# One wait per transpose, one signal per normalisation, and a mask tile moved by 64 bytes

## The reference, cut to what matters

```python
h = jnp.maximum(_layernorm(x, axis=-1), 0.0)
# _direction, for each relation r of a direction:
#   sum_r (adj == r) @ ((h W.T + b_r) * sigmoid(h W.T Wg.T + bg_r))
out = _direction(h, W_fwd, Wg_fwd, ..., adj, rels)             # relations 2 to 40
out = out + _direction(h, W_bwd, Wg_bwd, ..., adj_t, rels)
out = out + _direction(h, W_loop, Wg_loop, ..., adj_t, rel1)   # relation 1
return x + jax.nn.relu(out)
```

## Time and profile before

| | |
|---|---|
| median of three runs | 104.29 us (104.07 to 104.54) |
| the profiled execution's own time | 104.14 us |
| its span | 102.4 us |
| TensorE clock | full speed, 0.999 of it |
| PE busy | 96.5 us, 94% |
| DVE busy | 90.3 us, 88% |
| ACT busy | 90.3 us, 88% |
| POOL busy | 83.8 us, 82% |

### The profile page before, as it was taken

One profiled execution on the slowest core, in us unless ns is written; L12 is line 12 of the kernel. 1 busy time (PEld: TensorE's weight loads), 2 busy tenths in 40 slices (PEclk: granted clock), 3 DMA queues, 4 the chain that ended last, 5 costly groups with the idle time before them and its releaser, 6 DMA issues.

```text
span 102.4 us, 2495 instructions
## 1 busy us (share of the span) xinstructions
PE 96.5 (94%) x802; PEld 92.5 (90%) x802; DVE 90.3 (88%) x197; ACT 90.3 (88%) x148; POOL 83.8 (82%) x158
## 2 busy tenths in 40 slices
PE   5988899999999999999999999999999999999960
PEld 2657798999999999999999999999999999999950
DVE  2289899999999999999999999999998588877661
ACT  5068889989999999999999989998999989898890
POOL 2275999999999999999999999999999999960000
PEclk9999999999999999999999999999999999999999
DMA  2899999999999999999999999999933341506345
GB/s 63 249 313 292 293 290 290 293 294 288 274 313 304 321 321 324 301 324 333 335 328 333 317 339 322 304 312 312 315 100 109 92 113 55 156 15 197 102 137 170
DMA packets 50288, 25.45 MB, mean 249 GB/s; under 512 B 866, under 2 KB 50276, under 8 KB 50276
## 3 DMA queue, kind: packets, MB, share of 16 engines
q1 hardware_dynamic: 50000, 25.17, 88.0%
q10 hardware_dynamic: 276, 0.13, 0.4%
HBM read 16.91 MB, written 8.39 MB: 247 GB/s over the span
## 4 chain that ended last, share of the span: by engine, by line
PE 80%; DMA 7%; DVE 4%; SPq 3%; ACT 3%; issue 1%
PE psum L827 25%; PE psum L805 14%; PE psum L806 14%; PE psum L810 14%; PE psum L792 13%; DMA x_all<-in_x 7%; ACT junk L467 2%; SPq L253 2%; DVE stats L554 1%; DVE xn L571 1%; DVE vals L587 1%; DVE hT_lo L597 1%; SPq L269 0%; SPq L270 0%; ACT gate L461 0%
## 5 line engine op out<-in xcount | busy, mean ns | idle before, releaser
L366 POOL TENSOR_SCALAR xn<-x_all,mean_neg,rstd 128x128 f32<-128x128 f32 x96 | 42.4, 456 | 0.5 <-issue 0.3
L805 PE MATMUL psum<-w_hi,hT_hi 128*128 128x256 f32 x128 | 34.3, 301 | 0.7 <-ACT hT_hi L427 0.3
L434 ACT ACTIVATE psum<-bias_all 128x1024 f32<-128x1024 f32 x32 | 33.0, 1032 | 0.7 <-DVE vals L587 0.6
L827 PE MATMUL psum<-vals,mask 128*128 128x128 f32 x256 | 33.6, 275 | 0.0
L806 PE MATMUL psum<-w_lo,hT_hi 128*128 128x256 f32 x128 | 31.6, 280 | 0.0
L827 PEld LDWEIGHTS psum<-vals,mask 128*128 128x128 f32 x256 | 31.1, 191 | 0.0
L554 DVE BATCH_NORM_STATS2 stats<-x_all 128x6 f32<-128x256 f32 x64 | 24.0, 420 | 3.5 <-DMA x_all<-in_x 3.5
L587 DVE TENSOR_TENSOR vals<-psum,gate 128x512 f32<-128x512 f32 (+1 forms) x33 | 21.9, 665 | 4.0 <-ACT gate L461 3.8
L805 PEld LDWEIGHTS psum<-w_hi,hT_hi 128*128 128x128 f32 x128 | 24.1, 188 | 1.5 <-issue 0.9
L348 POOL TENSOR_TENSOR rstd<-var_eps,minus_half 128x16 f32<-128x16 f32 (+2 forms) x11 | 24.5, 2224 | 0.1
L806 PEld LDWEIGHTS psum<-w_lo,hT_hi 128*128 128x128 f32 x128 | 24.2, 189 | 0.0
(11 more groups left out here) (38 smaller groups left out, 34.5 us busy)
## 6 DMA issues: line engine op xcount, KB each, us to landing
adj_all<-in_adj SPq DMA_DIRECT2D x16, 512.0 KB, 6.5
x_all<-in_x SPq DMA_DIRECT2D x15, 512.0 KB, 6.7
out<-x_all SPq DMA_DIRECT2D x14, 512.0 KB, 6.3
out<-x_all SPq DMA_DIRECT2D x3, 256.0 KB, 2.3
x_all<-in_x SPq DMA_DIRECT2D x2, 256.0 KB, 3.0
out<-x_all ACTq DMA_DIRECT2D x1, 128.0 KB, 2.5
out<-x_all SPq DMA_DIRECT2D x1, 128.0 KB, 2.6
w_raw<-in_L_gnn_W_loop SPq DMA_DIRECT2D x1, 64.0 KB, 2.4
```

The source lines that it names most:

```text
L366: last = pool.tensor_scalar(xn[:, g % XN, j * D:j * D + D], x_all[:, g * GC + j * D:g * GC + j * D + D], mean_neg[:, b % BATCH_SLOTS, k:k ...
L434: nc.scalar.activation(prod_ps[s].rearrange("p g a d -> p g (a d)"), bias_all[:, :, :].rearrange("p a d -> p (a d)").unsqueeze(1) .to_broa ...
L805: nc.tensor.matmul(to, hi, w_hi[:, :], start=False, stop=False, skip_group_check=True)
L827: last = nc.tensor.matmul(to[:, j * D:j * D + D], mask[:, g % MASKS, j * N:j * N + N], vals[:, s, j * D:j * D + D], start=True, stop=True)
```

## The change

Three things change.

1. Every normalisation instruction signals, on all three engines, and the counters count graphs: `pool_groups` and `dve_groups` become `pool_graphs` and `dve_graphs`, sums of the shares.
2. In `turn_rows` each transpose waits for its own graph's normalisation. The wait for the PSUM slot now comes first. The graphs of VectorE (or ScalarE) are transposed first, those of GpSimd last.
3. `minus_half` is allocated behind `mean_neg`. So `mask`, `stats`, `var_eps`, `rstd` and `mean_neg` move down by 64 bytes and begin at multiples of 128; what lies behind stays where it was.

```diff
-        minus_half = sb("minus_half", [128, BATCH])
         mask = sb("mask", [128, MASKS, GROUP * N])
...
         mean_neg = sb("mean_neg", [128, BATCH_SLOTS, BATCH])
+        minus_half = sb("minus_half", [128, BATCH])
...
-        def pool_groups(g):
-            return sum(pool_share(k) > 0 for k in range(g))
+        def pool_graphs(g):
+            return sum(pool_share(k) for k in range(g))
...
-                    last = pool.tensor_scalar(
+                    pool.tensor_scalar(
                         xn[:, g % XN, j * D:j * D + D], x_all[:, g * GC + j * D:g * GC + j * D + D],
                         mean_neg[:, b % BATCH_SLOTS, k:k + 1], rstd[:, b % BATCH_SLOTS, k:k + 1],
-                        ALU.add, ALU.mult)
-                last.then_inc(normed_pool, 1)
+                        ALU.add, ALU.mult).then_inc(normed_pool, 1)
...
             def turn_rows(g):
                 s = g % 2
-                if pool_share(g) > 0:
-                    pe.wait_ge(normed_pool, pool_groups(g + 1))
-                if g == ACT_GROUP:
-                    pe.wait_ge(normed_act, 1)
-                if dve_share(g) > 0:
-                    pe.wait_ge(normed_dve, dve_groups(g + 1))
                 if g >= 2:
                     pe.wait_ge(hT_ready, g - 1)
-                for j in range(GROUP):
+                for j in [*range(pool_share(g), GROUP), *range(pool_share(g))]:
+                    if j < pool_share(g):
+                        pe.wait_ge(normed_pool, pool_graphs(g) + j + 1)
+                    elif g == ACT_GROUP:
+                        pe.wait_ge(normed_act, j + 1)
+                    else:
+                        pe.wait_ge(normed_dve, dve_graphs(g) + j - pool_share(g) + 1)
                     last = nc.tensor.transpose(hT_ps[s][:, j * N:j * N + N], xn[:, g % XN, j * D:j * D + D],
                                                ident[:, :])
                 last.then_inc(turned, 1)
```

More of the change, by code:

```diff
@@ L219, in pool_share, with dve_graphs @@
             return POOL_SHARES[g] if g < len(POOL_SHARES) else BATCH_SHARES[g - batch_of(g)[1]]
-        def pool_groups(g):
-            return sum(pool_share(k) > 0 for k in range(g))
+        def pool_graphs(g):
+            return sum(pool_share(k) for k in range(g))
         def dve_share(g):
             return 0 if g == ACT_GROUP else GROUP - pool_share(g)
-        def dve_groups(g):
-            return sum(dve_share(k) > 0 for k in range(g))
+        def dve_graphs(g):
+            return sum(dve_share(k) for k in range(g))
         def means_before(b):
@@ L340, in coefficients @@
                 if b >= BATCH_SLOTS:
-                    pool.wait_ge(normed_dve, dve_groups(BATCHES[b - BATCH_SLOTS][1] + 1))
+                    pool.wait_ge(normed_dve, dve_graphs(BATCHES[b - BATCH_SLOTS][1] + 1))
                 pool.tensor_scalar(var_eps[:, s, 0:n].rearrange("p (k e) -> p k e", e=2), st[:, :, :, 2],
@@ L445, in normalise @@
                     at = ACT_GROUP * GC + j * D
-                    last = nc.scalar.activation(
+                    nc.scalar.activation(
                         xn[:, ACT_GROUP % XN, j * D:j * D + D], x_all[:, at:at + D], ACT.Identity,
-                        bias=shift[:, j:j + 1], scale=rstd[:, b % BATCH_SLOTS, j:j + 1])
-                last.then_inc(normed_act, 1)
+                        bias=shift[:, j:j + 1], scale=rstd[:, b % BATCH_SLOTS, j:j + 1]).then_inc(normed_act, 1)
             def sigmoid(g):
@@ L562, in normalise @@
                 b, first, _ = batch_of(g)
-                if dve_groups(g) == dve_groups(first):
+                if dve_graphs(g) == dve_graphs(first):
                     dve.wait_ge(rstd_ready, b + 1)
@@ L570, in normalise @@
                     mean = stats[:, b % BATCH_SLOTS, k // 2, 1 + k % 2 * 3:2 + k % 2 * 3]
-                    last = nc.vector.tensor_scalar(
+                    nc.vector.tensor_scalar(
                         xn[:, g % XN, j * D:j * D + D], x_all[:, g * GC + j * D:g * GC + j * D + D],
-                        mean, rstd[:, b % BATCH_SLOTS, k:k + 1], ALU.subtract, ALU.mult)
-                last.then_inc(normed_dve, 1)
+                        mean, rstd[:, b % BATCH_SLOTS, k:k + 1], ALU.subtract, ALU.mult).then_inc(normed_dve, 1)
             def messages(g):
```

## The result

| | before | after |
|---|---|---|
| median | 104.14 us (103.74 to 105.74, 8 runs) | 103.36 us (103.24 to 103.52, 8 runs) |
| ratio | | 0.9923, 95% interval 0.9911 to 0.9935 |
| profiled execution, span | 104.14, 102.4 us | 103.40, 101.6 us |
| PE, DVE, ACT, POOL busy | 96.5, 90.3, 90.3, 83.8 us | 95.9, 90.4, 90.9, 83.9 us |

A forecast was written before the change was run, and what follows sets the result against it. TensorE, busy 94% of the span, was taken to bound the kernel. All terms were 0, so 104.14 + 0 = 104.14, predicted as 104.2 us, range 103.7 to 104.8.

The forecast's parts named there:

- The masks' address: Aggregation passes with `mask` as weights: moving it to a multiple of 128 gains 0; by the row's difference 0.32 us.
- rival B: The masks' address speeds up the aggregation's passes: 103.9 us, or 103.55 if they gained twice that; chance 0.10.
- This head start ends where two queues wait for transfers.: Groups 0 and 1: up to 0.33 us earlier, lost waiting for x and adj; value 0, bounds 0 to -0.30.
- Group 3: Transposes end 0.33 us earlier, but products wait for `seed(2)`: idle 0.32 becomes 0.65; value 0.
- Group 6: Products start 0.06 us earlier, then `aggregate(4)` waits for `messages(4)`; value 0, bound -0.22.
- Signals and satisfied waits: GpSimd's and VectorE's new signals and the transposes' already satisfied waits cost nothing; bound 0.03 us a wait.
- Rivals C and D: C: a wait amid transposes costs TensorE its beat, at most 2.8 us, 0.08; D: signals slow GpSimd, 104.9 us, 0.02.
- Rival A: Head starts of groups 3 (0.33) and 6 (0.22) survive: 103.65 us; chance 0.07.
- Behind 26.91. Nobody waits there.: Steady groups from 26.91 us on: TensorE is full at 2.742 us each, so finer waits gain nothing; value 0.

The follow-up runs named there:

- e0_before_again: The kernel before, unchanged, profiled once more: 104.92 us, measured once.
- e6_all_128: The kernel after with 64 bytes of padding ahead of `ident`, so all TensorE operands of the steady part begin at multiples of 128: 104.34 us, ratio 1.001.
- h1_vals_64: The kernel before with `minus_half` ahead of `vals`, which moves only `vals` up by 64 bytes: 104.73 us, ratio 1.0009.
- h3_mask_only_again: The kernel before with `mask` alone moved to a multiple of 128, measured once more: 103.58 us, ratio 0.9909.
- e3_signals: The kernel before with the new signals alone; transposes wait for the whole group, old order and addresses: 104.51 us, ratio 1.0013.
- j1_w_192: The kernel before with `ident`, `w_hi`, `w_lo` and `bias_all` moved up by 192 bytes: 104.47 us, ratio 1.0027.
- j2_waits_w_128: The kernel before with the new waits and signals, and `ident`, `w_hi`, `w_lo`, `bias_all` 128 bytes up: 103.38 us, ratio 0.9931.
- e2_waits: The kernel after with `minus_half` back ahead of `mask`: new waits and signals at the old addresses; 103.96 us, ratio 0.9975.
- e7_hT_64: The kernel after with `hT_hi` and `hT_lo` moved to 64 over a multiple of 128: 104.24 us, ratio 0.9984.

## Why the prediction was wrong, point by point

**The step that failed: "The masks' address ... I take 0."** I looked for the effect in the passes whose operand moved, where 1.25 ns on 256 passes bounded it at 0.32, and rival B rested on the same row. Those passes did not change: 0.89 for eight in both kernels. The products did, 1.41 to 1.36 for twelve. I had used their row only as the far bound of a loss, "with nothing that speaks for it, as its weights lie at a multiple of 128 too". That is true of `hT_hi`, the product's weight operand, and leaves out the other side: its moving operand `w_hi` lies 64 over, and the runs show that the relative place of the two is worth up to 2.753 - 2.706 = 0.047 us a group. Of the product's 6.25 ns above the aggregation's pass some 4 were room for a gain; 24 x 0.05 = 1.2 us were to be had, and 0.40 were kept.

The rule that I weighed, from the Trainium skill (SBUF — State Buffer, section on the DMA port swizzle), would have left the time at 104.2. The Trainium skill says there that each access that crosses to a new 16-byte line pays a penalty; that nothing else is penalised was my reading. The runs don't agree with that reading: all moves here were multiples of 64 bytes, so every tile began such a line before and after, and the ratio went from 1.0027 to 0.9869.

**"This head start ends where two queues wait for transfers."** This failed too. The start of after:
```profile
7.33 0.54 PEld L789 LDWEIGHTS psum<-ident,xn 128*128 128x128 f32 x4
...
8.17 0.59 ACT L425 ACTIVATE hT_hi<-psum 128x512 fp32r<-128x512 f32 x1
...
12.62 0.64 ACT L416 ACTIVATE mask<-adj_all 128x512 f32<-128x512 int32 x1 [0.42 <-DMA adj_all<-in_adj]
...
13.49 0.60 ACT L458 ACTIVATE gate<-psum 128x512 f32<-128x512 f32 x1 [0.23 <-PE psum L807]
...
14.46 1.04 ACT L432 ACTIVATE psum<-bias_all 128x1024 f32<-128x1024 f32 x1
14.51 0.47 PEld L789 LDWEIGHTS psum<-ident,xn 128*128 128x128 f32 x4
...
15.61 0.19 PEld L802 LDWEIGHTS psum<-w_hi,hT_hi 128*128 128x128 f32 x1 [0.63 <-issue]
```
`relu_turned(0)` starts 0.26 earlier, within the 0.33 I gave. `edges(0)` ends at 13.26, and `sigmoid(1)` starts only at 13.49, released by the products of group 1, which had moved up with the head start. The loads of the last four of those products, in after and in e0_before_again, followed by `edges(0)` in e6_all_128:
```profile
12.70 0.54 PEld L807 LDWEIGHTS psum<-w_hi,hT_lo 128*128 128x128 f32 x4
```
```profile
13.13 0.54 PEld L810 LDWEIGHTS psum<-w_hi,hT_lo 128*128 128x128 f32 x4
```
```profile
13.46 0.63 ACT L417 ACTIVATE mask<-adj_all 128x512 f32<-128x512 int32 x1 [0.98 <-DMA adj_all<-in_adj]
```
`sigmoid(1)` stands 0.79 behind in both (12.70 and 13.49, 13.13 and 13.92). In the trace of before that load is at 12.98; 0.79 more is 13.77, and `sigmoid(1)` starts at 13.79. Two chains met there, the transfer with `edges(0)` and the products of group 1. I saw the idle time ahead of `edges(0)` and did not ask what `sigmoid(1)` behind it waited for. With that, 14.74 became 14.46. The step as I had it does occur where the transfer lands late: in e6_all_128, with the new waits, `edges(0)` idles 0.98 (I had forecast 1.07) and group 4 starts at 18.68. Over all profiles in which the chain shows it, group 4 starts at 18.46 to 18.79 with the old waits (nine, median 18.55) and at 18.16 to 18.68 with the new (nine, median 18.27).

**Group 3: right.** The loads of the four transposes begin at 14.51, before VectorE's last graph, and the first product stands 15.61 - (14.46 + 1.04) = 0.11 behind the end of `seed(2)`. I had forecast 0.65 of idle time in place of 0.32; it is 0.63.

**Group 6: right in this pair, too narrow in general.** Group 6 of after:
```profile
22.94 0.60 DVE L568 TENSOR_SCALAR xn<-x_all,stats,rstd 128x128 f32<-128x128 f32 x2
...
23.40 0.51 PEld L789 LDWEIGHTS psum<-ident,xn 128*128 128x128 f32 x4
...
24.74 0.67 DVE L583 TENSOR_TENSOR vals<-psum,gate 128x512 f32<-128x512 f32 x1
...
25.48 0.97 PEld L824 LDWEIGHTS psum<-vals,mask 128*128 128x128 f32 x8
```
The aggregation comes 0.07 behind the end of `messages(4)` and all of it is 0.27 earlier, which is the start's gain. In other executions there was more to lose. With the old waits group 6's transposes stood 3.04 instead of 2.74 behind group 5's in three profiles of eleven (e0_before_again, h1_vals_64, h3_mask_only_again), and in e3_signals, whose chain doesn't show group 5, they waited 0.41 for GpSimd. In four (e0_before_again, e3_signals, h1_vals_64, j1_w_192) group 30 started 2.90 to 2.97 behind group 29. There VectorE's normalisation ran beside two casts on GpSimd, and the transposes came 0.07 behind its end; from e0_before_again:
```profile
88.99 1.50 DVE L571 TENSOR_SCALAR xn<-x_all,stats,rstd 128x128 f32<-128x128 f32 x1
89.24 1.16 POOL L377 CAST mask<-adj_all 128x512 f32<-128x512 int32 x2
...
90.56 0.42 PEld L792 LDWEIGHTS psum<-ident,xn 128*128 128x128 f32 x4 [0.33 <-issue]
```
None of the nine profiles with the new waits shows this at group 30, though at group 6 in j2_waits_w_128 the last transpose waited 0.30 for GpSimd. Whether the waits prevent it isn't shown: they can't shorten an instruction of VectorE, and several profiles with the old waits don't have it either.

**Signals and satisfied waits: right.** GpSimd's batches with the signals are 10.77 in the mean (e3_signals), four transposes take 0.44 in both kernels, and e2_waits has the period of before. Rivals C and D are out.

**Rival A** gave 0.55 for the head starts of groups 3 and 6. About half of that came, from groups 0 and 1, which A did not hold.

**"Behind 26.91. Nobody waits there."** It was true, and the wrong conclusion was drawn: where one engine is full, its beat is a term of the sum, and 0.05 a group counts 24 times. I had named another period behind 26.91 as the sign of being wrong, and it came. The ceiling was there to be read, too: GpSimd's 10.84 a batch and VectorE's 10.99 busy of 11 us were close behind TensorE's 10.97, and `seed`, behind VectorE's `messages`, held TensorE as soon as it became faster.

In sum: the waits start group 7 earlier by 0.27 to 0.29 (after and e2_waits against before; 0.28 in the medians of group 4's start, whose ranges overlap). The place of `mask` alone gives a ratio of 0.9895 to 0.9909. Together they give less than their sum in some series and about it in one; what the waits add on top of the address lies between nothing and 0.3 us. The forecast was off by 0.84 us, and by the trace's own terms 0.40 of the 0.80 that the span lost come from the address, 0.27 from the start and 0.13 from behind group 31. For the last I had no term, and no run takes it apart.

**Open.** Why the place of `mask` acts on the products. The records show only that the fast beat comes in stretches of several groups and that the group in which TensorE had to wait is slow. I have no run that reaches the cause, nor one that says which tile the place of `mask` is relative to. Nor is it shown why the two distances of 64 and 192 differ, and what makes GpSimd's batch 10.7 to 10.9 long from one execution to the next.

## What to carry to other kernels

Where one engine is busy without a gap, compare the beats of its like instructions to the nanosecond before calling the stretch fixed, and try a few relative places of the operands in SBUF: a pad of 128 bytes gave as much here as the whole change. Don't take aligning every tile for the best: in this kernel it was as slow as any version, and a product's operands 64 bytes apart modulo 128 were faster. Measure it in yours. When idle time in front of an instruction is put down to a transfer, ask what the next instruction on that engine waits for, too: an equally late chain may stand right behind it. And before you count a gain per group, see how far behind the next engine is.

## What the runs showed of the hardware that was not expected

- The same fp32r products, 256 columns wide, took 12 x 113 ns (1.36), 114 ns (1.37), 117.5 ns (1.41) or 118 ns (1.42), by the places in SBUF alone. The clock was 0.992 to 1.0 in all of these.
- The slow case is that of equal offsets modulo 128 (2.753 a group in e6_all_128, e7_hT_64 and j1_w_192), and aligning everything produces it.
- A tile that the products don't read (`mask`) changed their beat, 2.742 to 2.693 a group, but only at one of the distances: at 192 the two places of `mask` gave 2.707 and 2.709.
- VectorE's normalisation of one graph, 0.34 at 88.55 in the trace of before, beside GpSimd's own normalisations, took 1.50 in e0_before_again at 88.99, and ended 0.09 behind the two casts that GpSimd ran meanwhile.
